# A ring of one-hots with packed tables, one Block for adjacency and convolution, and f32 queries in a graph kernel

## What is computed

```python
# convolution, with self loops added to src and dst
h = leaky(batchnorm(x @ W1 + b1)); h = h / norm(h)
for _ in range(5):
    m = h @ W
    agg = segment_sum(m[src] * (dinv[src] * dinv[dst])[:, None], dst) + bias
    h = leaky(batchnorm(agg))
x = layernorm(x + h / norm(h))
# attention, 8 heads of 16
Q, K, V = x @ wq + bq, x @ wk + bk, x @ wv + bv
scores = ((Q[src] * K[dst]).sum(-1) + (Q[src] * (edge_attr @ we + be)).sum(-1)) / 4
es = exp(scores); w = es / (segment_sum(es, src)[src] + 1e-8)
x = layernorm(x + segment_sum(w * V[dst], src) @ wo + bo)
```

## Time and profile before

| | us |
|---|---|
| median of 3 runs (lowest, highest) | 5244.65 (5244.09, 5247.79) |
| the profiled execution | 5247.15 |
| its span | 5245.6 |
| preparation (0 to 283) | 283 |
| adjacency build (283 to 1447) | 1164 |
| end of it, start of the convolution (to 1553) | 106 |
| five rounds (to 2994) | 1441 |
| normalise, project (to 3111) | 117 |
| attention (to 5170) | 2059 |
| output projection and the end | 76 |

### The profile page before, as it was taken

One profiled execution on the slowest core, in us unless ns is written; L12 is line 12 of the kernel. 1 busy time (PEld: TensorE's weight loads), 2 busy tenths in 40 slices (PEclk: granted clock), 3 DMA queues, 4 the chain that ended last, 5 costly groups with the idle time before them and its releaser, 6 DMA issues. The chain is left out here.

```text
span 5245.6 us, 95577 instructions
## 1 busy us (share of the span) xinstructions
PE 3828.0 (73%) x24852; PEld 2425.0 (46%) x24853; DVE 3410.0 (65%) x10241; ACT 1665.9 (32%) x4208; POOL 3435.8 (65%) x3648
## 2 busy tenths in 40 slices
PE   5346666666639999999999857676666667676664
PEld 3112222222224454545454436666666666666664
DVE  8999999999921120202020168887887878878787
ACT  0056666666620010101010123333333333333332
POOL 2067777777777777777730017777777777777773
PEclk8889999999969999999999979999999999999998
DMA  9322332322379999898978634444444444444442
GB/s 365 119 85 92 102 128 90 139 90 95 134 185 327 321 310 336 295 337 290 337 270 291 197 105 131 131 131 131 132 132 131 131 130 131 132 131 132 131 131 77
DMA packets 363179, 929.25 MB, mean 177 GB/s; under 512 B 75929, under 2 KB 193549, under 8 KB 361192
## 3 DMA queue, kind: packets, MB, share of 16 engines
q1 hardware_dynamic: 203136, 552.41, 31.6%
q0 software_dynamic: 143520, 317.62, 21.4%
q10 hardware_dynamic: 16400, 57.93, 2.9%
HBM read 727.27 MB, written 200.43 MB: 177 GB/s over the span
## 5 line engine op out<-in xcount | busy, mean ns | idle before, releaser
L749 POOL DMA_INDIRECT records<-recs,poss x1562 | 1626.5, 1041 | 552.8 <-issue 544.0
L1380 POOL DMA_INDIRECT kv<-kv_table,rec x1616 | 1552.5, 961 | 497.4 <-issue 465.4
L909 PE MATMUL ps<-adj,mh 128*128 128x500 f16 (+1 forms) x6370 | 1315.4, 366 | 0.0
L1418 PE MATMUL ps<-msg,ohf 128*128 128x136 f32 x3232 | 504.1, 301 | 636.8 <-DVE msg L1478 635.5
L582 PE MATMUL ps<-h 128*128 128x490 f16 x2500 | 651.5, 385 | 399.4 <-ACT h L683 342.0
L909 PEld LDWEIGHTS ps<-adj,mh 128*128 128x128 f16 x6370 | 619.8, 97 | 686.4 <-issue 35.8
L1063 DVE SCALAR_TENSOR_TENSOR h<-ps,vecs,deg (+1 forms) x65 | 46.7, 718 | 1120.3 <-PE ps L909 1120.3
L537 DVE TENSOR_SCALAR h<-iota,rel 128x490 f16<-128x490 f16 x2500 | 774.0, 370 | 0.0
L1418 PEld LDWEIGHTS ps<-msg,ohf 128*128 128x128 f32 x3232 | 418.8, 196 | 712.8 <-DVE msg L1478 364.4
L582 PEld LDWEIGHTS ps<-h 128*128 128x128 f16 x2500 | 200.7, 99 | 850.3 <-ACT h L683 555.8
L1444 ACT ACTIVATE msg<-scores 128x32 f32<-128x32 f32 x404 | 92.6, 229 | 1288.8 <-DVE scores L1473 1288.8
(11 more groups left out here) (262 smaller groups left out, 4519.6 us busy)
## 6 DMA issues: line engine op xcount, KB each, us to landing
adj<-adj_full SPq DMA_DIRECT2D x420, 875.0 KB, 5.9
adj_full<-blk SPq DMA_DIRECT2D x12, 6125.0 KB
records<-deg ACTq DMA_DIRECT2D x1, 56576.0 KB, 198.1
rec<-records SPq DMA_DIRECT2D x404, 136.0 KB
recs<-in_edge_attr POOLq DMA_DIRECT2D x142, 352.0 KB, 5.6
kv<-kv_table,rec POOLq DMA_INDIRECT x1616
records<-recs,poss POOLq DMA_INDIRECT x1563
adj<-adj_tail SPq DMA_DIRECT2D x35, 437.5 KB, 3.7
```

Source lines behind the costliest of these rows:

```text
L749: G.indirect_dma_start(out=k.rec_d, out_offset=bass.IndirectOffsetOnAxis(ap=k.poss[:, q, j:j + 1], axis=0), in_=k.recs[:, q, j, :], in_off ...
L909: last = mm(bank, mh[:, part, hi, :], adj[:, c, x * width:(x + 1) * width], start=False, stop=True, skip_group_check=True)
L1380: G.indirect_dma_start(out=kv[:, q, j, :], out_offset=None, in_=k.kv_d, in_offset=bass.IndirectOffsetOnAxis(ap=rec[:, q, j, RD:RD + 1].bit ...
L1418: last = mm(PS[:, 6 + q % S, j // 2 * MW:(j // 2 + 1) * MW], ohf[:, q, j, :], msg[:, q, j, :], start=(j % 2 == 0), stop=(j % 2 == 1))
```

## The change

- `ohl` becomes a ring of 50 slots (RING), one per tile, so that each tile's one-hot is made once and read by every window that needs it. Three slots stand twice, at the ring's start and past its end, so that four neighbours are always contiguous. Of each 12.5 new tiles in a group ScalarE makes six in three pairs (two distances and one Relu over both), VectorE the rest (`spread`). VectorE's `ohc` compare a fixed range of codes with `k.code` directly, since the codes now count within four windows (PH); L528 and L517 are gone.
- The table has one word for VectorE (the first tile and four steps of 3 bits) and one for TensorE (five ring positions of 6 bits). ScalarE needs no table. TensorE's weight address comes from a register.
- ScalarE no longer waits for its own put; TensorE waits on the put itself.
- The window table is made from running extremes (two scans) and counts instead of masks; ScalarE counts the ends.
- `adjacency` returns its five programs and `convolve` runs them at its start, in one Block: the other engines wait for SyncE's `graph_stored`, GpSimd for nothing. GpSimd scatters in one run, in two buffers of 22 columns, and fetches the next step after five scatters of a step (FETCH).
- The degrees are stored block by block from `degs`.
- Q stays in f32 (`k.qn`), and each of the twelve query products becomes one f32 product per tile, four a group; `oht` is f32.

```diff
-                        for x in range(WPP):
-                            last = V.tensor_scalar(rel[:, par, x, :], k.code[:, bass.ds(first[x], FAST)], wbase[:, bass.ds(w + x, 1)], None, ALU.subtract)
-                        for x in range(WPP):
-                            q = (q0 + x) % SL
-                            v.wait_ge(done, w + x + 1)
-                            lo_onehots(ohl[:, q, 0:JV[x], :], first[x], JV[x])
-                            for j in range(FAST):
-                                last = V.tensor_scalar(ohc[:, q, j, :], iota[:, :], rel[:, par, x, j:j + 1], None, ALU.is_equal)
+            def spread(t, i=None):
+                slot = t % RING
+                of_tile = k.lo[:, t:t + 1] if i is None else k.lo[:, bass.ds(i * (2 * TWO) + t, 1)]
+                for q in (slot, slot + RING) if slot < FAST - 1 else (slot,):
+                    V.tensor_scalar(ohl[:, q * P:(q + 1) * P], codes[:, 0:P], of_tile, None, ALU.is_equal)
...
+                packed = entry(nc, DVE, k.wt, gr * TW + DWORD, 0, 2 * DLONG)
+                with v.If(packed < DLONG):
+                    first = v.snap(within(packed >> 12, T - FAST))
+                    for x in range(WPP):
+                        q, f = (w0 + x) % SL, (w0 + x) % PH
+                        if x:
+                            first = v.snap(within(first + ((packed >> (12 - 3 * x)) & 7), T - FAST))
+                        v.wait_ge(done, w + x + 1)
+                        for j in range(FAST):
+                            last = V.tensor_scalar(ohc[:, q, j, :], codes[:, f * WC:(f + 1) * WC], k.code[:, bass.ds(first + j, 1)], None, ALU.is_equal)
...
+                pe.wait_ge(ready_lo, gr * PAIRS + PAIRS)
...
-                                last = nc.tensor.matmul(PS[:, q, 0:WC], ohl[:, q, j, :], ohc[:, q, j, :],
+                                last = nc.tensor.matmul(PS[:, q, 0:WC], ohl[:, bass.ds(at + j * P, P)], ohc[:, q, j, :],
...
-                    A.activation(a[:, :, x * WD:(x + 1) * WD],
-                                 PS[:, (q * BW + x) % SL, 0:WC].rearrange("p (h d) -> p h d", h=NB),
-                                 ACT.Copy, scale=0.25).then_inc(put, 1)
-                    act.wait_ge(put, w + 1)
-                    act.sem_inc(psum_free, 1)
+                A.activation(blk[:, q, :].rearrange("p (h d) -> p h d", h=NB)[:, :, y * WD:(y + 1) * WD],
+                             PS[:, slot, 0:WC].rearrange("p (h d) -> p h d", d=WD), ACT.Copy, scale=0.25).then_inc(put, 1)
+            def distances(t, i, n):
+                for j in range(2):
+                    last = A.activation(away[:, n, j, :], codes[:, 0:P], ACT.Abs, bias=of_tile, scale=-1.0)
+            def onehots(t, n, nth):
+                A.activation(ohl[:, slot * P:(slot + 2) * P], away[:, n, :, :].rearrange("p j c -> p (j c)"), ACT.Relu, bias=1.0, scale=-1.0).then_inc(ready_lo, 1)
...
+                sp.dma_start(k.deg_d[bass.ds(b * BD, width)].rearrange("(o c) -> o c", o=1), degs[0:1, q, 0:width]).then_inc(deg_moved[q], 16)
...
-                nc.gpsimd.memset(onesf[:], 1.0).then_inc(consts, 1)
-                scatter_records(k, g, SPLIT, NS // RR)
+                pool_adj(g)
...
-                sp.wait_ge(padded, 1)
-                sp.dma_start(k.deg_d.rearrange("(p c) -> p c", p=1), k.deg[0:1, :]).then_inc(deg_moved, 16)
-                sp.wait_ge(deg_moved, 16)
+                sp_adj(sp)
+                sp.wait_ge(stored, 1)
...
+                pe_adj(pe)
+                pe.wait_ge(stored, 1)
...
-                    V.tensor_tensor(qs[:, x % QS, 0:m, :], PS[:, 4 + t % 4:4 + t % 4 + m, 0:D], spread(bqkv[:, 0, :], m), ALU.add)
+                    V.tensor_tensor(k.qn[:, t:t + m, :], PS[:, 4 + t % 4:4 + t % 4 + m, 0:D], spread(bqkv[:, 0, :], m), ALU.add)
...
-                        for part in range(3):
-                            mm(PS[:, 2 + q % S, j * P:(j + 1) * P], oht[:, q % S, j, :],
-                               k.q3[:, bass.ds(b[j // 2], 1), part, :].rearrange("p a c -> p (a c)"), start=(part == 0), stop=(part == 2))
+                        mm(PS[:, 2 + q % S, j * P:(j + 1) * P], oht[:, q % S, j, :],
+                           k.qn[:, bass.ds(b[j // 2], 1), :].rearrange("p a c -> p (a c)"), start=True, stop=True)
```

659 lines of the change are left out of this document (349 added, 310 removed).

## The result

| | kernel before | changed kernel |
|---|---|---|
| median of 4 runs, us | 5246.22 | 5128.94 |
| lowest, highest | 5244.09, 5249.86 | 5122.28, 5136.97 |
| ratio | | 0.9776 (95%: 0.9759 to 0.9793) |
| profiled execution | 5247.15 | 5122.28 |

A forecast was written before the change was run, and what follows sets the result against it. VectorE was taken to bound the adjacency build, TensorE the rounds, GpSimd the attention. Savings 239 + 6 - 4 + 13 + 2 = 256 took 5247.15 to 4991, or 4989 us at the median; range 4905 to 5090.

The forecast's parts named there:

- The work of a group: Adjacency build, VectorE, five windows: 20 wide compares at 0.257 us and 7.3 new-tile compares at 0.17 make 6.4 us.
- What wasn't hidden: Adjacency build, VectorE: 0.2 us per group for register steps and table load, and 25 us idle kept of 56 before.
- Interference: Adjacency build: GpSimd's scatters cost VectorE 0.13 us each, five in a group, 0.6 us per group.
- GpSimd starved: Rival: VectorE's compares block all scatters in the build, so they end at 3346; 5574 us in all; chance 0.03.
- The rule that I set against the trace of before: Build: single-input compares in two-port mode fully block GpSimd, two-input instructions only meet its reads; VectorE's new stream would starve it.
- The scatters' rate outside the build: GpSimd: a step of 22 scatters takes 30.2 us, from 0.968 + 0.30 a scatter and 2.3 a step.
- The start: Before the build: window table 6 us shorter, block start 4 us later through a larger iota and 15 one-hots.
- the end of the build: Tail's store to first input product: 40.6 us against 53.8, 13 us saved, bounds 5 and 15.
- project: Project stage: queries in f32 drop copies and subtractions; 2 us saved, bounds 0 and 8.
- rounds and attention: Both unchanged: rounds of 289 us, and attention groups of 5.06 us set by GpSimd's gathers; nothing saved.
- VectorE is held by its register steps: Rival, build: register steps and additions cost 2.05 us per group, 0.05 each, and cancel the 256 us; chance 0.05.
- TensorE becomes the bound: Rival, build: unhidden weight loads at 0.1 us raise TensorE's group to 8.2 us; 125 us more, 5114; chance 0.13.

The follow-up runs named there:

- the run without scatters: Changed kernel, loop of 4 groups, with GpSimd waiting for the whole matrix to be stored before its first scatter; 5682.6 us in a single run.
- the loops of 8 and 20: Changed kernel plus one register step, VectorE's build loop turning once per 8 or 20 groups instead of 4; 5048.2 us with 8, 5005.4 us with 20.
- the disturbed condition: Four of seven groups of runs, nothing changed on purpose; the kernel before took 6297 to 6636 us, most variants of the changed one 7553 to 7726.

## Why the prediction was wrong

- **The work of a group: right.** 6.4 us without interference; the run without scatters had 6.42. With them 6.9 (860 / 125); outside the stops a group took (1058 - 171) / 125 = 7.1, forecast 7.2.
- **What wasn't hidden: the step that failed.** "56 us before, about 4.5 us at each of 12 block changes", of which the sum keeps 25 us. The idle time before wasn't at block changes: VectorE's waits there are at L528 for TensorE (22.7 us in 13) and for "issue" (18.6 in 10), and at L517 (9.6 in 12), none over 2.7 us. The term left out what a turn of VectorE's own loop costs. In the changed kernel that is two stops at each of 30 turns, 171 us in place of 25. That is 146 us too little, and the group's 0.1 us less gives 12 of it back: the build came out 137 us above the forecast. No row of the kernel before shows such a cost, for its loop turned as often and went on 0.24 us after each branch. The count of turns is shown to be the cause by the loops of 8 and 20. That the turn became dear because a pass grew from 199 to 281 instructions is the reading that fits, and no run tests it: none shortened the pass.
- **A rule that spoke of this and that I didn't weigh.** In the changed kernel's trace a turn costs two stops of 2.0 and 2.1 us with one compare between them. The Trainium skill, Runtime: NRT & Kernel Launch, section Instruction fetch mechanics, says that an engine holds its instructions in a queue of two 16 KiB blocks, filled ahead in order and by DMA, and that a taken branch to a place outside the two has to wait for a fetch. By that rule a loop's turn is such a branch whenever the loop is longer than the two blocks. The trace agrees as far as it goes: three packets of 8 KB a turn, later ones where a block's store is under way, and no stop in the shorter loop of the kernel before. The lengths of the loops in bytes are not in the trace. The same section calls the crossing of a block boundary mostly hidden; within the loop of 20 hardly any such stops are seen, so the trace agrees with that as well.
- **Interference: right in size, by another way.** 0.46 us a group against 0.6. It is not five scatters at 0.13 each but two kinds of group: in one a scatter waits for the whole group and VectorE loses nothing (a window each 1.03 us), in the other four or five get through (1.23).
- **GpSimd starved: the mechanism was there, in part.** I gave it 0.03 and a price only if complete. The rule that I set against the trace of before (the Trainium skill, SBUF — State Buffer, section Who interferes with whom) came true for 73 of 515 scatters: the stream of wide f16 compares with one input held them off for up to 6.1 us, and beside the two-input L517 none took over 1.72. It did not for all: in other groups scatters got through between the same compares, and the short f16 compares with one input didn't hold them. The row that I held against the rule, 1.34 us under L517, was of a scatter that got through. It cost nothing in the changed kernel, as the build was late too. It cost 58 us as soon as that was mended, and 18 of these came back by moving the last scatters.
- **The scatters' rate outside the build: right.** 1047 scatters in the 1421 us from 1338 to 2759 are 1.36 each; the forecast was 30.2 / 22 = 1.37.
- **The start, the end of the build, project, rounds and attention: right**, within 5, 0.4, 1.1, 1.5 and 0.9 us.
- **VectorE is held by its register steps: not seen**, the group's work came out as summed. The price in that rival is off: 2.05 us over 35 register steps and additions are 0.06 us each, not 0.05.
- **TensorE becomes the bound: not seen**, though its forecast of 5114 is closest to the result. A hit of a number is no evidence: in the loop of 20 TensorE is busy for 755 of 894 us, VectorE for 860.
- **With the one wrong term mended**, in the loop of 20, the sum goes as it was made: its build is 32 us shorter than the 925 of the forecast and its start 5 us earlier, and the scatters hold the Block for 58, which the forecast had covered; 4989 - 32 - 5 + 58 = 5010, and 5005 were measured.

## What to carry to other kernels

When a change makes the body of a long loop longer, look in the trace at that engine's branches, before and after. Here the same loop with the same 31 passes turned for nothing with 199 instructions in a pass and stopped VectorE for 4 us a turn with 281, and for up to 9 more beside a large store. Fewer turns, the loop over 20 groups in place of 4, were worth more than the whole change: 138 us against 117. When the instruction that breaks up a stream of wide one-input f16 compares leaves VectorE, look at what GpSimd does beside it: it may only get through at the stream's breaks. And when an engine is busy for 81% and its idle time is put down to "issue", ask where in the program it stands: here it stood at every turn of a loop, with packets of instructions beside it, while in the disturbed condition VectorE lost 532 us to the same word in a build that waited for late semaphores.

## What the runs showed of the hardware

- A turn of a loop with 281 instructions in a pass stops VectorE twice, 2.0 and 2.1 us, with a single instruction between; 31, 15 and 6 passes gave 171, 83 and 15 us. A turn of the loop with 199 cost no stop.
- Each such turn brings three 8 KB packets on the instruction queue (233, 185 and 159 packets on the pages).
- Of six turns that met a 6 MB store well under way (10 to 12 us after it went out) five had a first stop of 8.8 to 9.6 us, which ended 0.3 to 0.6 us after the store's landing, and one a stop of 7.0 us, which ended before it; stores that had just gone out cost a stop 0.9 us at most.
- 73 of 515 scatters of GpSimd that met f16 compares of 490 columns and one input took 5.65 us in the mean, against 0.97 alone, and all but one of the others under 1.5; with a 16-column two-input instruction in each fifth of the stream none took over 1.95. 38 of the 73 ended 0.24 or 0.95 us after short one-input compares began, as did 57 of 66 in the loop of 20.
- The same kernel on the same chip took 6636 us in one group of runs and 5242 in another. In the slow one everything beside GpSimd's indirect DMAs slows down, and goes at its usual rate as soon as they end (135 and 1198 VectorE instructions in 300 us).
